# A selective-scan block with a mixture of experts: the gate of a chunk moved from VectorE to ScalarE and GpSimd

## The reference

```python
xi, z = split(layernorm(x) @ W_in)              # 256 channels each
u = silu(causal_conv4(xi) + conv_b)
delta, Bm, Cm = ...                             # from u; state size 64
h = h * exp(delta_t * A) + (delta_t * u_t) * B_t     # a scan over 1024 tokens
y = einsum(h, C_t) + u * D
y = y * silu(z)                                 # the gate
x = layernorm(2 * x + y @ W_out)
x = layernorm(x + moe(x))                       # 4 layers, 4 experts, top 2
```

## Time and profile before

| | us |
|---|---|
| median of 3 runs | 2173.34 (2171.91 to 2173.38) |
| the profiled execution, its own time | 2171.85 |
| its span in the profile | 2170.0 |
| VectorE busy over the span | 1834.1 (85%) |
| ScalarE busy | 1619.6 (75%) |
| GpSimd busy | 957.0 (44%) |
| TensorE busy | 2111.8 (97%) |
| first scan starts, last gate of the scans starts | 154.83, 1315.33 |

### The profile page before, as it was taken

One profiled execution on the slowest core, in us unless ns is written; L12 is line 12 of the kernel. 1 busy time (PEld: TensorE's weight loads), 2 busy tenths in 40 slices (PEclk: granted clock), 3 DMA queues, 4 the chain that ended last, 5 costly groups with the idle time before them and its releaser, 6 DMA issues.

```text
span 2170.0 us, 50688 instructions
## 1 busy us (share of the span) xinstructions
PE 2111.8 (97%) x16984; PEld 1254.2 (58%) x16984; DVE 1834.1 (85%) x2692; ACT 1619.6 (75%) x2288; POOL 957.0 (44%) x457
## 2 busy tenths in 40 slices
PE   7979999999999999999999998999999999999998
PEld 3432333333333333333333336899999999999998
DVE  6889999999999999999999997656755565666675
ACT  5888999999999999999999995444555554554553
POOL 3124344444344434443444343544544454455542
PEclk9988999999999999999999999999999999999999
DMA  5884222121212121212121225000200010000000
GB/s 178 287 298 139 49 42 49 40 49 41 48 41 49 40 49 40 49 41 48 40 49 40 49 73 161 31 0 0 64 1 0 0 64 1 0 0 6 10 10 15
DMA packets 310765, 118.85 MB, mean 55 GB/s; under 512 B 258520, under 2 KB 290400, under 8 KB 310048
## 3 DMA queue, kind: packets, MB, share of 16 engines
q1 hardware_dynamic: 306224, 114.85, 20.0%
q10 hardware_dynamic: 4464, 3.02, 0.4%
HBM read 71.91 MB, written 45.88 MB: 54 GB/s over the span
## 4 chain that ended last, share of the span: by engine, by line
PE 57%; DVE 17%; issue 14%; ACT 9%; POOL 2%; DVEq 0%; ACTq 0%; DMA 0%; SPq 0%; POOLq 0%
PE PS L1414 20%; PE PS L1402 16%; DVE arena L1637 14%; PE PS L1308 8%; ACT behind L1027 7%; PE PS L1291 4%; PE PS L1265 4%; PE PS L1188 1%; PE PS L1391 1%; PE PS L1320 1%; PE PS L1322 1%; PE PS L1234 1%; ACT behind L1015 1%; PE PS L1225 1%; DVE arena L1477 0%
## 5 line engine op out<-in xcount | busy, mean ns | idle before, releaser
L1637 DVE TENSOR_TENSOR_SCAN arena<-behind 128x1040 f32<-128x1040 f32 x512 | 1145.0, 2298 | 4.1 <-ACT behind L1027 1.7
L1155 ACT ACTIVATE arena<-PS,arena 128x512 f32<-128x512 f32 x512 | 343.6, 688 | 390.4 <-PE PS L1402 390.0
L1015 ACT ACTIVATE behind<-PS 128x1024 f32<-128x1024 f32 x512 | 527.0, 1029 | 84.7 <-PE PS L1265 41.7
L1308 PE MATMUL PS<-arena 128*32 128x128 f32 x8192 | 566.2, 406 | 0.0
L1027 ACT ACTIVATE behind<-PS 128x1024 f32<-128x1024 f32 (+2 forms) x640 | 547.0, 879 | 7.9 <-PE PS L1291 0.9
L1414 PEld LDWEIGHTS PS<-arena 128*128 128x128 f32 x4096 | 473.0, 192 | 7.5
L1414 PE MATMUL PS<-arena 128*128 128x128 f32 x4096 | 473.6, 275 | 0.0
L826 POOL COPY behind<-carry 128x64 f32<-128x64 f32 x128 | 233.7, 1828 | 475.0 <-DVE arena L1637 334.8
L1308 PEld LDWEIGHTS PS<-arena 128*32 128x32 f32 x8192 | 234.9, 119 | 287.5 <-issue 212.1
L1402 PE MATMUL PS<-parts_xh,parts_w 128*128 128x512 f32 x1536 | 378.1, 397 | 8.9 <-ACT arena L1155 6.2
L1785 DVE SCALAR_TENSOR_TENSOR arena<-PS,arena 128x128 f32 (+1 forms) x508 | 142.9, 344 | 228.4 <-PE PS L1414 227.3
(11 more groups left out here) (143 smaller groups left out, 1433.0 us busy)
## 6 DMA issues: line engine op xcount, KB each, us to landing
dl_d<-arena SPq DMA_DIRECT2D x48, 256.0 KB, 3.2
du_d<-arena SPq DMA_DIRECT2D x48, 256.0 KB, 3.2
arena<-dl_d SPq DMA_DIRECT2D x512, 24.0 KB
arena<-b_d SPq DMA_DIRECT2D x64, 192.0 KB
arena<-du_d SPq DMA_DIRECT2D x512, 24.0 KB
b_d<-arena SPq DMA_DIRECT2D x48, 128.0 KB, 1.9
u_d<-behind SPq DMA_DIRECT2D x8, 512.0 KB, 3.9
sz_d<-arena SPq DMA_DIRECT2D x8, 512.0 KB, 4.8
```

The costliest lines, as they stand in the source:

```text
L1015: nc.scalar.activation(seg(dA[:, half])[:, :, 1:], PS[:, 0:2, :].rearrange("p j (i t) -> p (j i) t", t=TC), ACT.Exp).then_inc(exp_done, 1)
L1155: nc.scalar.activation(hT[:, e % 2, c], PS[:, HIDDEN[(GT * e + c) % 3], :], ACT.Gelu, bias=bias1[:, lp, e * GT + c:e * GT + c + 1]).then_i ...
L1308: last = nc.tensor.matmul(PS[32 * j:32 * j + 32, 4 + kk, 0:DB], cd[:, pair, j, 32 * i:32 * i + 32], seg(hb[kk])[:, :, 1 + 16 * j + i], sta ...
L1637: nc.vector.tensor_tensor_scan(hb[kk][:, q * QD * SEG:(q + 1) * QD * SEG], dA[:, q % 2], dB[:, G_, lo:lo + QD * SEG], 0.0, ALU.mult, ALU.a ...
```

## The change

The gate of chunks 0 to 30 no longer runs on VectorE. Its place in VectorE's list, behind the last scan of a chunk, is empty. ScalarE gets a copy at the same step of its own list: the turned outputs go from PSUM to `G`, 128 partitions by 256 elements (`lift`, new semaphore `g_lifted`). GpSimd then multiplies `G` in place by `silu(z)` and posts `g_done` (a new `gate` in its list, behind the `slots` for the next block). The gate of chunk 31 stays on VectorE.

```diff
@@ gpsimd @@
+            def gate(m):
+
+                pool.wait_ge(g_lifted, m + 1)
+                apart(pool)
+                parts = lambda v: v.rearrange("p h (t b) -> p h t b", b=2)
+                nc.gpsimd.tensor_tensor(parts(G), parts(G), usz_of(m)[:, 1].rearrange("p h b t -> p h t b"), ALU.mult
+                                        ).then_inc(g_done, 1)
+
@@ gpsimd, emit @@
                     slots(2 * blk + 2, nc_, np_, nk, 0)
+                if kk == 1 and held(chunk):
+                    gate(chunk - 1)
@@ scalar @@
+            def lift(m):
+
+                act.wait_ge(post_t, m + 1)
+                apart(act)
+                nc.scalar.activation(G, turned_both(m).rearrange("p (h t) -> p h t", h=HALVES), ACT.Identity
+                                     ).then_inc(g_lifted, 1)
+
@@ scalar, emit, each step q @@
+                    if q == Q_GATE and kk == 1 and held(chunk):
+                        lift(chunk - 1)
@@ vector, emit, each step q @@
-                    if q == Q_GATE and kk == 1 and held(chunk):
-                        gate(chunk - 1)
```

More of the change, by code:

```diff
@@ L360, in build @@
         g_done = sem("g_done")
+        g_lifted = sem("g_lifted")
         out_ready = sem("out_ready")
```

## The result

The changed kernel takes 2186.88 us (median of 4 runs, 2186.31 to 2188.12) where the one before takes 2173.36: a ratio of 1.0062, 95% interval 1.0047 to 1.0077. It is 13.5 us slower. The forecast was slower by 6.9 us, with a range up to 2185.0; the direction was right, the size was half of what came, and the time lies above the range.

The account below looks back on a forecast made before the run. VectorE, which never waits in the scans, was taken to bound the kernel. A hold of 0.58 less 0.35 us regained is +0.23 us a gate, +6.9 for 30: 2173.34 + 6.9 = 2180.2 us, range 2172 to 2185.

Parts of the forecast that it names:

- What bounds the kernel: In the scans VectorE never waits: what enters or holds its list lengthens the stage, what leaves shortens it.
- The hold: GpSimd's multiplication at each chunk's start keeps VectorE's next scan from reading memory: a loss of 0.58 us a gate.
- the high end: GpSimd's multiplication with the step on silu(z) paid in full: 220 ns more, 765 ns for 256 columns, loss 0.66 us.
- the estimate beside it: From the Trainium skill's cycles a column, GpSimd's stepped read costs 213 ns for 256 columns; sum near +9 us.
- the rule "end less start less 0.175": A held VectorE scan, issued 0.075 us early behind another, loses the GpSimd instruction's end less the scan's start, less 0.175.
- The range given for the stepped read: Forecast's own range, with GpSimd's stepped read of silu(z) paid half to wholly: 2177.7 to 2184 us.
- The gate that goes: At chunk ends VectorE's next scan starts 0.315 us sooner without the gate: 30 x 0.315 = 9.5 us gained.
- The small copy: GpSimd's copy under the gate no longer runs into a chunk's first scans: 0.035 us a gate gained on the mean.
- ScalarE, GpSimd's wait, the end: ScalarE's added copy, GpSimd's copies queued behind the multiplication, and the last chunk's late copy: each costed at nothing.
- A: Rival: same hold on VectorE's scans with cheap reads, 0.35 to 0.48 us a gate, 2173.3 to 2177.3 us; chance 0.26.
- B: Rival: no hold on VectorE's scans and the gate hidden, all 10.5 us come back, 2162.8 us; chance 0.09.
- C: Rival: ScalarE's copy also makes it late, or the stepped operand costs more than a stepped write; 2185 and up; chance 0.05.

## Why the prediction was right and wrong

**What bounds the kernel:** right for what is put into VectorE's list or holds it up: that came out at the end. Wrong for what is taken out, as told below.

**The hold:** right in mechanism and in size: 0.58 us a gate forecast, 0.56 measured, 16.9 us in all for 17.4. Added alone to the old kernel it costs the same. Its parts were less right. The columns took 2.36 ns each (the instruction ends 0.59 us after the scan it waited for, and by the prediction's count 0.01 more goes to them), not 2.70. The step of 64 elements costs 0.07 us for 256 columns, a third of the 0.22 by which the high end was made, and of the 213 ns of the estimate beside it: a price from a stepped write in a one-input copy does not hold for this read in a two-input instruction. And the loss was 0.56 where the rule "end less start less 0.175" makes 0.50 of the measured end. The two errors nearly cancelled, so that the size came out so close is in part luck. The range given for the stepped read does not follow either: half to wholly paid makes 2179.2 to 2182.6 us, and 2177.7 to 2184 is that with 1.5 us on each side, which the text does not say. The 296 ns in the price of the stepped write is 292 in the earlier trace rows; that moves the high end by 0.015 us.

**The gate that goes:** this is the step that failed. "30 x 0.315 = 9.5 us" came out as 2.8, and the missing 6.7 us are what the forecast was short by (6.9 for 13.5). The prediction read in the earlier trace rows that VectorE has no idle time and took it that the next scan could start 0.315 us sooner. That no engine waits says only that what it waits for is not late, not by how much it is early. TensorE's sums of states two blocks back, for which the first scan of a block waits (`y_done`), ended 0.20 us before that scan: 412.22 + 1.11 = 413.33 by the trace of before, against 413.53. They must be 0.07 to 0.12 us ahead, as the gaps show, so the gate had 0.1 us to give back. TensorE's turn, 0.9 us one step ahead, stands only at the chunks' ends: between the two blocks of a chunk, where there is none, the same sums end 0.53 us ahead of the scan. With the sums shortened the wait is gone and the 9.5 us are there, in both kernels. With 2.8 for 9.5 and the prediction's own other terms, the sum is 17.4 - 2.8 - 1.1 = 13.5 us.

The row that would have told it, TensorE's timeline of the kernel before at the chunk's end of the earlier trace rows, and below it the sums between that chunk's two blocks, ahead of a scan that starts at 431.59:

```profile
412.22 1.11 PE L1308 MATMUL PS<-arena 128*32 128x128 f32 x16
...
429.95 1.11 PE L1308 MATMUL PS<-arena 128*32 128x128 f32 x16
```

The prediction followed ScalarE's exponentials ahead of the scans and found 0.5 us of slack. It did not follow the other semaphores of the scan behind the gate, though the order of the kernels lists all five.

**The small copy:** its 0.035 us a gate came out as 0.6 us in all for the first scans (1.1 forecast). A first scan that starts behind a gap takes 0.03 us more (2.325 us in the changed kernel); in the two kernels with shorter sums, where there is no gap, it takes 2.293 and the first scans give back 1.3.

**ScalarE, GpSimd's wait, the end:** right. The copy took 0.38 us and the idle time before the exponential behind it went from 0.46 to 0.20; by the profile no scan waits for an exponential. The last copy waited 1.62 us for TensorE's turn and made nothing late.

**The rivals:** A (0 to +4 us) put the hold at 0.35 to 0.48 us, under the 0.56 measured, and shared the price of the gate that goes. B, that the hold is not there, is refuted by the multiplication added alone. C, at 2185 and up, has the measured time in it, but by another way: it named ScalarE as the late engine, and it was TensorE, on the side of the gain. The prediction's last sign of being wrong, idle time of VectorE behind ScalarE, did show by the profile's name (4.2 us, of which 2.6 put down to ScalarE's copy); the experiments show that the name is not the cause.

## What to carry to other kernels

When an instruction is taken from the list of the engine that never waits, look at each semaphore of the next instruction and at how long before it the last one was posted: the smallest of these slacks bounds what can come back. A wait of several semaphores is not to be read by the name that the profile gives; shorten one suspected producer and nothing else, and see whether the gap goes. And work moved from VectorE to GpSimd is not off VectorE while VectorE scans with both operands in memory: here it cost 0.56 us where the gate had cost 0.32.

## What the runs showed of the hardware

- A VectorE scan with two operands in memory was held by a two-input float32 multiplication on GpSimd: by 0.56 us for 256 columns and 0.26 for 128, 2.4 ns a column. VectorE's gate, with one operand in PSUM, ran beside it at its usual 0.39 us.
- GpSimd's fixed part (0.19 us) is spent while it waits: a multiplication that was held ended 0.59 us after the scan for 256 columns and 0.29 for 128, which leaves nothing for a fixed part. It cost the next scan 0.03 us less than that. Held copies of 64 columns ended 0.10 us after the scan and cost nothing.
- One of two inputs read in pairs 64 elements apart, and not in a row, costs GpSimd 0.28 ns a column (0.072 us for 256; one trace of each).
- VectorE started 0.07 to 0.12 us after the last matmul that it waited for had ended, by the profile's model of matmul ends, in four kernels. In the kernel with the sums ahead of the products, behind ScalarE's copy, it started 0.3 us after the first piece (the copy's 0.39 us taken from the earlier trace rows).
